# Expert results of a mixture-of-experts layer: written to their tokens' places and read back as blocks, in place of block writes and row gathers

## What is computed

```python
shared = silu(X @ sW1 + sb1) @ sW2 + sb2
activation = sqrt(softplus(X @ routing_W + expert_bias))
top_vals, top_idx = top_k(activation, 2)
y_e = silu(X @ rW1[e] + rb1[e]) @ rW2[e] + rb2[e]
out = layernorm(X + shared + sum of top_vals * y_e over the token's two experts)
```

## Time and profile before

| what | before |
|---|---|
| median of three runs | 2392.36 us |
| profiled execution, its own time | 2394.0 us |
| its span in the trace | 2392.2 us |
| PE busy | 2230.7 us (93%) |
| DVE busy | 1534.3 us (64%) |
| ACT busy | 883.9 us (37%) |
| POOL busy | 1113.8 us (47%) |
| moved by DMA | 233.26 MB |

### The profile page before, as it was taken

One profiled execution on the slowest core, in us unless ns is written; L12 is line 12 of the kernel. 1 busy time (PEld: TensorE's weight loads), 2 busy tenths in 40 slices (PEclk: granted clock), 3 DMA queues, 4 the chain that ended last, 5 costly groups with the idle time before them and its releaser, 6 DMA issues.

```text
span 2392.2 us, 40085 instructions
## 1 busy us (share of the span) xinstructions
PE 2230.7 (93%) x13154; PEld 1939.7 (81%) x13154; DVE 1534.3 (64%) x3594; ACT 883.9 (37%) x1887; POOL 1113.8 (47%) x1061
## 2 busy tenths in 40 slices
PE   6999999999999999999999999999869999999860
PEld 5788888888888878888888887888759999989750
DVE  5655666655556667655556667665656545888886
ACT  3333333333333333333333333333346555555420
POOL 1233343433333334644445453356355453777776
PEclk9999999999999999999999999999979999999995
DMA  4011111111111111111111111111264455998996
GB/s 164 18 41 49 36 36 45 45 36 41 49 36 36 36 45 36 45 36 41 49 36 36 45 45 36 36 36 37 93 212 151 152 154 179 307 312 298 298 310 209
DMA packets 102486, 233.26 MB, mean 98 GB/s; under 512 B 18256, under 2 KB 18768, under 8 KB 101520
## 3 DMA queue, kind: packets, MB, share of 16 engines
q1 hardware_dynamic: 75744, 157.96, 18.5%
q0 software_dynamic: 26256, 72.71, 10.5%
q10 hardware_dynamic: 288, 0.04, 0.0%
HBM read 141.11 MB, written 89.53 MB: 96 GB/s over the span
## 4 chain that ended last, share of the span: by engine, by line
PE 82%; DVE 6%; POOL 4%; issue 4%; DMA 3%; ACT 1%; SPq 0%; DVEq 0%; POOLq 0%; ACTq 0%
PE banks L107 23%; PE banks L109 23%; PE banks L108 23%; PE banks L113 7%; POOL RG L1811 2%; PE banks L709 2%; DMA RG<-ys,POS 1%; PE banks L447 1%; PE banks L546 1%; PE banks L731 1%; POOL b_small L1683 1%; DMA ys<-b_Y 1%; POOL b_XN L1799 1%; DVE xc L1055 1%; DVE W L1052 1%
## 5 line engine op out<-in xcount | busy, mean ns | idle before, releaser
L107 PE MATMUL banks<-W 128*128 128x512 f32 (+1 forms) x2040 | 752.9, 369 | 15.9 <-DVE W L1052 15.9
L109 PE MATMUL banks<-W 128*128 128x512 f32 (+1 forms) x2040 | 717.8, 352 | 0.0
L108 PE MATMUL banks<-W 128*128 128x512 f32 (+1 forms) x2040 | 716.6, 351 | 0.0
L107 PEld LDWEIGHTS banks<-W 128*128 128x128 f32 x2040 | 388.5, 190 | 67.7 <-POOL W L1683 15.0
L109 PEld LDWEIGHTS banks<-W 128*128 128x128 f32 x2040 | 387.2, 190 | 54.0
L108 PEld LDWEIGHTS banks<-W 128*128 128x128 f32 x2040 | 388.7, 191 | 50.7 <-issue 7.2
L772 ACT ACTIVATE W<-banks 128x512 fp32r<-128x512 f32 x320 | 191.0, 597 | 521.3 <-DVE banks L1052 243.3
L1683 POOL TENSOR_TENSOR W<-S,W 128x512 fp32r<-128x512 f32 x256 | 327.8, 1306 | 117.3 <-ACT W L772 117.2
L1683 POOL TENSOR_TENSOR X<-X,B 128x1024 f32<-128x1024 f32 x32 | 78.8, 2464 | 620.6 <-DMA X<-in_x 620.6
L772 ACT ACTIVATE W<-S 128x512 fp32r<-128x512 f32 (+1 forms) x288 | 180.4, 650 | 227.8 <-DVE S L1052 211.8
L1052 DVE TENSOR_TENSOR W<-banks,W 128x512 fp32r<-128x512 f32 x192 | 132.2, 688 | 172.3 <-ACT W L772 172.3
(11 more groups left out here) (156 smaller groups left out, 4433.6 us busy)
## 6 DMA issues: line engine op xcount, KB each, us to landing
ys<-b_Y SPq DMA_DIRECT2D x149, 256.0 KB
XT<-in_xT SPq DMA_DIRECT2D x32, 512.0 KB, 3.5
X<-in_x SPq DMA_DIRECT2D x32, 512.0 KB, 3.5
x1d<-X SPq DMA_DIRECT2D x64, 256.0 KB, 2.0
zd<-X SPq DMA_DIRECT2D x64, 256.0 KB, 2.0
b_Y<-zd SPq DMA_DIRECT2D x64, 256.0 KB, 5.1
out<-b_Y SPq DMA_DIRECT2D x64, 256.0 KB, 4.4
S<-in_we SPq DMA_DIRECT2D x32, 256.0 KB, 4.6
```

The lines of the kernel that those rows point to most:

```text
L107: e.matmul(o, ll, rh, start=start, stop=False, skip_group_check=True)
L108: e.matmul(o, lh, rl, start=False, stop=False, skip_group_check=True)
L109: return e.matmul(o, lh, rh, start=False, stop=stop, skip_group_check=True)
```

## The change

1. `ys` is one array: two planes of 64 x 128 rows (a row for each token, one plane for its first expert, one for its second) and behind them 149 x 128 spare rows. What POOL scatters into `ids` is now the place of the result, plane times 8192 plus the token's number (`idt` has two columns of numbers for it). An unfilled position of a slot holds the number of a spare row, put there at the start by DMAs out of an input array (`spare`) in place of zeros from SBUF.
2. `load` needs token numbers. `tokens(g)` works them out of `IDX`, with three small POOL instructions for a group, in front of the group's first load (i = 0, 63 and 118).
3. The write of a slot's result moves from SP (`store`) to POOL (`send(i-2)`): an indirect DMA that scatters `Y`'s rows to their places.
4. The two gathers of an ending move from POOL to SP (`rows`): two plain DMAs of 128 x 512 blocks. They wait for the same things as before, now on SP, between `fetch` and `store_out`.
5. Group 1's scatters in steps 29 and 30 go from six tiles each to eight; so eight of its tiles are left for phase two, not twelve.

```diff
@@ -28,7 +28,7 @@
 NL = len(LEVELS)
 NCST = 3
 GROUPS = [14, 12, 6]
-SCATTERS = [[3] * 10, [6, 6]]
+SCATTERS = [[3] * 10, [8, 8]]
...
-    k.ys = [nc.dram_tensor(f"ys{g['x']}", (g["slots"] * P, D), F32, kind="Internal").ap() for g in k.groups]
+    k.ys = nc.dram_tensor("ys", ((2 * NTL + k.n_slots) * P, D), F32, kind="Internal").ap()
...
+        k.EX, k.IDX, k.idt = sb("EX", [k.n_slots], I32), sb("IDX", [k.n_slots], I32), sb("idt", [2, NTL], I32)
+        k.TOK = sb("TOK", [k.n_slots], I32)
...
-            e.indirect_dma_start(k.ids[g["x"]], off, k.idt[:, n:n + 1], None).then_inc(k.d_scatter.sem(m), 16)
+            e.indirect_dma_start(k.ids[g["x"]], off, k.idt[:, j, n:n + 1], None).then_inc(k.d_scatter.sem(m), 16)
...
-    w.wait_ge(k.s_lev, 2)
-    w.wait_ge(k.s_ones, 1)
-    e.memset(k.RG[:, 0:k.n_slots], 0.0).then_inc(k.s_zero, 1)
...
 
+    def tokens(g):
+
+        a = slice(g["slot"], g["slot"] + g["slots"])
+        w.wait_ge(*k.d_idx.of(g["x"]))
+        n, x = k.NTL * P, 3 * g["x"]
+        e.tensor_scalar(k.TOK[:, a], k.IDX[:, a], float(n), float(-n), ALU.is_ge, ALU.mult).then_inc(k.s_tok, 1)
+        w.wait_ge(k.s_tok, x + 1)
+        tt(k.TOK[:, a], k.TOK[:, a], k.IDX[:, a], ALU.add).then_inc(k.s_tok, 1)
+        w.wait_ge(k.s_tok, x + 2)
+        e.tensor_scalar(k.TOK[:, a], k.TOK[:, a], float(n - 1), None, ALU.min).then_inc(k.s_tok, 1)
+
     def load(i):
 
         if i >= N:
             return
         g = k.items[i]
-        w.wait_ge(*k.d_idx.of(g["x"]))
+        if i == g["slot"]:
+            tokens(g)
+        w.wait_ge(k.s_tok, 3 * g["x"] + 3)
         for s, v in k.d_x1.last(g["tile"] + g["tiles"]):
             w.wait_ge(s, v)
         w.wait_ge(k.s_tp, i - XNS + 1)
@@ -1795,20 +1806,18 @@
             w.wait_ge(*split_of(k, 24 + i))
         else:
             w.wait_ge(k.s_dn1, k.NTL)
+        off = bass.IndirectOffsetOnAxis(ap=k.TOK[:, i:i + 1], axis=0)
+        e.indirect_dma_start(k.XN[i % XNS][:], None, k.x1d, off).then_inc(k.d_xs.sem(i), 16)
+
+    def send(i):
+
+        if not 0 <= i < N:
+            return
+        w.wait_ge(*k.d_idx.of(k.items[i]["x"]))
+        w.wait_ge(k.s_Y, i + 1)
+        w.wait_ge(*k.d_y.of(i - 3))
         off = bass.IndirectOffsetOnAxis(ap=k.IDX[:, i:i + 1], axis=0)
-        e.indirect_dma_start(k.XN[i % XNS][:], None, k.x1d, off).then_inc(k.d_xs.sem(i), 16)
-
-    def gather(c):
-        f = k.plan.finals[c]
-        w.wait_ge(k.s_cm, 4 * (c - 2) + 2)
-        for s, v in k.d_y.last(f.g["slot"] + f.g["slots"]):
-            w.wait_ge(s, v)
-        w.wait_ge(k.s_rt, k.rt_after["pos", last["x"]])
-        for j in range(2):
-            m = 2 * c + j
-            w.wait_ge(*k.d_gather.of(m - 4))
-            off = bass.IndirectOffsetOnAxis(ap=k.POS[:, j, f.n, :], axis=0)
-            e.indirect_dma_start(k.G[j][c % 2], None, k.ys[f.g["x"]], off).then_inc(k.d_gather.sem(m), 16)
+        e.indirect_dma_start(k.ys, off, k.Y[k.plan.buffer["item", i]][:], None).then_inc(k.d_y.sem(i), 16)
 
     def root(c):
         i = c % 2
@@ -1834,8 +1843,7 @@
         load(i + 6)
         if i - 3 in k.plan.base:
             root(k.plan.base[i - 3])
-        if i in k.plan.base:
-            gather(k.plan.base[i])
+        send(i - 2)
         if i == 24:
             weights(last)
         if i in k.plan.scatter:
...
-    w.wait_ge(k.s_zero, 1)
     for g in k.groups:
-        e.dma_start(k.ids[g["x"]].rearrange("(p s) o -> p (s o)", p=P), k.RG[:, 0:g["slots"]].bitcast(I32)).then_inc(k.d_zero, 16)
-    w.wait_ge(k.d_zero, 48)
+        e.dma_start(k.ids[g["x"]].rearrange("(p s) o -> p (s o)", p=P), a["spare"][:, g["slot"]:g["slot"] + g["slots"]]).then_inc(k.d_zero, 16)
+    w.wait_ge(k.s_lev, 2)
+    w.wait_ge(k.s_ones, 1)
     e.dma_start(k.RG[:, 0:KC * H + 2 * D], a["we"][E]).then_inc(k.d_sh, 16)
...
-    def store(i):
-        g = k.items[i]
-        w.wait_ge(k.s_Y, i + 1)
-        w.wait_ge(*k.d_y.of(i - 3))
-        rows = k.ys[g["x"]].rearrange("(p s) d -> p s d", p=P)[:, i - g["slot"], :]
-        e.dma_start(rows, k.Y[k.plan.buffer["item", i]][:]).then_inc(k.d_y.sem(i), 16)
+    def rows(c):
+
+        f = k.plan.finals[c]
+        w.wait_ge(k.s_cm, 4 * (c - 2) + 2)
+        for s, v in k.d_y.last(f.g["slot"] + f.g["slots"]):
+            w.wait_ge(s, v)
+        w.wait_ge(k.s_rt, k.rt_after["pos", k.groups[-1]["x"]])
+        for j in range(2):
+            m, at = 2 * c + j, (j * k.NTL + f.n) * P
+            w.wait_ge(*k.d_gather.of(m - 4))
+            e.dma_start(k.G[j][c % 2], k.ys[at:at + P, :]).then_inc(k.d_gather.sem(m), 16)
 
     def store_out(c):
         n = k.plan.finals[c].n
@@ -1960,8 +1973,7 @@
     for i in range(k.plan.end):
         if i in k.plan.base:
             fetch(k.plan.base[i])
-        if 0 <= i - 2 < N:
-            store(i - 2)
+            rows(k.plan.base[i])
         if i - 5 in k.plan.base:
...
-    arrays["ids"] = (np.arange(NB * NT)[None] * P + np.arange(P)[:, None]).astype(np.int32)
+    places = np.arange(2 * NB * NT)[None] * P + np.arange(P)[:, None]
+    arrays["ids"] = places.reshape(P, 2, NB * NT).astype(np.int32)
+    n_slots = groups_of(NT)[1]
+    arrays["spare"] = (2 * NB * NT * P + np.arange(n_slots)[None] * P + np.arange(P)[:, None]).astype(np.int32)
```

More of the change, by code:

```diff
@@ L197, in program @@
                   "rs", "X1", "X1hi", "X1lo", "LGc", "shhi", "shlo", "HF1", "hb1", "HS1", "HH1", "HL1", "dn1", "res", "z", "Sn", "Shi", "Slo", "B",
-                  "zero", "rt", "rta", "cum", "wt",
+                  "rt", "rta", "cum", "wt",
                   "whi", "w", "wp", "tp", "XH", "XL", "up", "HF", "hb", "HS", "HH", "HL", "dn", "Y",
-                  "cm", "crs", "o"):
+                  "cm", "crs", "o", "tok"):
             k.__setattr__("s_" + n, sem("s_" + n))
@@ L218, in program @@
         k.POS, k.WT = sb("POS", [2, NTL, 1], I32), sb("WT", [2, NTL])
-        k.EX, k.IDX, k.idt = sb("EX", [k.n_slots], I32), sb("IDX", [k.n_slots], I32), sb("idt", [NTL], I32)
+        k.EX, k.IDX, k.idt = sb("EX", [k.n_slots], I32), sb("IDX", [k.n_slots], I32), sb("idt", [2, NTL], I32)
+        k.TOK = sb("TOK", [k.n_slots], I32)
         k.mhalf = sb("mhalf", [2])
```

## The result

The changed kernel takes 2372.44 us, median of 4 runs (2370.23 to 2373.15), beside 2392.69 before (4 runs, 2389.82 to 2395.69): ratio 0.991, 95% interval 0.9898 to 0.9922. Compared again later, 2373.76 to 2390.87, ratio 0.9921 (0.9904 to 0.9938). The profiled span is 2368.4 against 2392.2, 23.8 us less.

The account below looks back on a forecast made before the run. PE was taken to bound (a) and (b), POOL's turn (c) and (d). Terms 0.4 + 0.2 - 5.9 + 1.9 - 5.3 = -8.7 took the median from 2392.36 to 2383.7 us, range 2374 to 2401.

Parts of the forecast that it names:

- (c): Slots of group 2 with endings of group 1: DMAs bind next at 4.75 us a slot; -5.9 us (0 to -12.5).
- the third rival: Scatter and plain reads are cheap for the DMAs, DVE alone binds (c); sum -17.3, 2375 us; chance 0.12.
- (d): Twelve endings of group 2 alone: 3.45 us each in place of 3.93, by latency; -5.3 us (-7.3 to 0).
- Last slot's step: From the last slot to group 2's first ending: 12.5 us in place of 10.6; +1.9 us (0 to +3.5).
- Tail: From the last scale to the end of the span: stays as it was, 0.
- (a) and (b): Slots alone, then group 1's slots with group 0's endings: PE stays the bound; 0 for each.
- (a): Slots alone: POOL falls 9 us behind with sends and tokens, under about 13 us of cover from early loads; 0.
- (b): Slots of group 1 with endings of group 0: PE stays the bound; 0 (-2.3 to +2).
- rival 2: Slower: the loop's send makes POOL the bound in (a) and (b); about 2401 us; chance 0.18.
- Steps 29 and 30: Two more tiles of scatters cost 5.1 us on POOL, mostly covered; +0.4 us (0 to +1).
- Start, tokens: Start: memset and waits removed beside the first products, 0; tokens: three small POOL instructions before the first load, +0.2 (0 to +1.1).
- Rival 1: The DMAs keep the pace in (c) and (d) and the gain is lost; about 2393 us (2389 to 2395); chance 0.20.

Follow-up runs that it names:

- x8: Changed kernel plus one unread plain write of 256 KB at each of group 1's 24 endings; stretch (c) 93.4 us, whole time not compared.
- x14: Changed kernel with the result scatter left out, SyncE storing each slot's result to a plain block; 2373.71 us, beside 2394.04 for the kernel before.
- x15: Changed kernel with the scaling of group 1's 24 endings done on 1 column of 512; 2370.27 us.
- x4: Changed kernel with the last 12 endings' root moved from POOL to ScalarE's square root and VectorE's reciprocal; 2484.24 us, in the slow conditions.
- x16: Changed kernel with scatters in steps 29 and 30 back to six and six tiles; 2377.61 us, beside 2394.04 for the kernel before.
- x11: Changed kernel with group 0's tokens made early and the last 12 endings' root off POOL; 2363.02 us, ratio 0.9881 to the kernel before.
- x13: Changed kernel with early tokens, late root off POOL, and a tile's two scatters of places in successive slots; 2476.63 us beside 2428.74 before.
- x9: The changed kernel itself, unaltered, run again for comparison; 2373.76 us against 2390.87 for the kernel before, ratio 0.9921.
- x1: Changed kernel with the result scatter left out, SyncE storing to plain blocks, in the slow conditions; stretch (c) 88.9 us, whole time not compared.
- x3: Changed kernel with plain stores from SyncE and group 1's scaling on 1 column, in the slow conditions; stretch (c) 87.2 us.

## Why the prediction was right or wrong

- *(c), -5.9 taken, -12.7 measured.* The step that failed is "So the DMAs bind next, and I take 4.75 us for a slot". The price of 3.43 us for 1 MB in the software queue was share divided by bytes; in the changed kernel's window from 2225 to 2265 us the same queue has 31.4% for 4.45 MB, 2.82 us: such a price is not fixed, and x8 moved a tenth more at the same share. DVE alone binds at 4.24 us a turn (x14, x15, x8), the case of the third rival: its -12.5 for (c) holds to 0.2 us.
- *(d), -5.3 taken, -6.4 measured.* 3.26 us an ending, the 3.27 of the earlier trace rows, which I had, and passed over for a sum of latencies. The root was the limit (x4: 2.91 without it). That it is not the -7.3 of the third rival comes from the first interval, 4.74 us.
- *Last slot's step, +1.9 taken, -0.9 measured.* The order of waits was right: the send starts 3.4 us after the result's end (2.9 taken). But it lands 3.6 us after its start, not 4.8 later, and the plain blocks, with little else moving, 2.5 us after issue, not 4.0. By the Trainium skill, DMA: Bandwidth & Descriptors, section Anatomy of one DMA, which is about software DMAs, the send's landing would be an estimate of 2.6 us; the trace doesn't agree. At 3.6 us it lies between that and the 4.8 of the rows. (2.2 us less than 4.8 make the whole sum -10.9, not the -11.1 that the prediction has.) In x14 the store was issued 2.0 us sooner after the result than the send, and landed 5.9 us after its issue: nothing won.
- *Tail, 0 taken, -3.1 measured.* "The end itself, last scale to the end, stays" is the second step that failed, a term put at nothing without a reason: POOL's closing DRAIN went from 9.60 to 6.50 us. It was not in my views, because they leave such instructions out. Only the gap of 9 us behind the last scale could have shown it.
- *(a) and (b), 0 taken, -1.9.* Cover and backlog in (a) are as worked out, 0.29 us of wait for PE; some slots at 59 to 62 cost about 1.1 us (x14). (b)'s 46 slots take 2.8 us less, 3.48 each, a little beyond the bound of -2.3 that I gave for 3.49. The send is 0.99 us and its gap 0.30, together 1.29 where I took 1.27; rival 2 needed a send of 1.5.
- *Steps 29 and 30, +0.4 taken.* DVE's addition in step 29 came 0.3 us later against its neighbours, and 0.1 or less was left by 1640 us; but what the edit is for escaped me (x16): I put a price on it and no worth.
- *Start, tokens +0.2 taken.* Tokens take 1.9 us where POOL had nothing else in hand; slot 0 comes 1.3 us later in one pair and 5.5 in the other. Matching ScalarE's instructions one by one shows that the first number is flattered: the changed kernel's trace was 3.4 us ahead at 100 us, the second pair's 0.2 behind. From there to slot 0 the change costs 4.7 and 5.3 us. 2.7 of them are lost between 908 and 917 us, in phase one, in a place that the prediction doesn't have, and 1.7 to 2.1 from 1740 us on, where the tokens stand. The scans of the routing on DVE, PE's wait behind them and the clock, in the changed kernel and then in x11:
```profile
901.26 2.71 DVE L1345 TENSOR_TENSOR_SCAN RG<-onesb,RG 128x28 f32<-128x28 bf16 x8
908.18 0.56 PE L107 MATMUL banks<-WS,X1l 128*128 128x264 f32 x1 [2.67 <-DVE X1l L1053]
895.00:925.00 30.00, 27.33 (x148) 23.29 (x147) 21.64 (x77) 7.94 (x17) 8.36 (x6) 0.94 0.08 27
...
901.73 1.33 DVE L1355 TENSOR_TENSOR_SCAN RG<-onesb,RG 128x28 f32<-128x28 bf16 x8
907.28 0.36 PE L108 MATMUL banks<-WS,X1l 128*128 128x264 f32 x1 [1.30 <-DVE X1l L1063]
895.00:925.00 30.00, 28.70 (x161) 24.25 (x161) 21.55 (x81) 8.48 (x19) 8.53 (x6) 1.00 0.10 36
```
The same eight scans take 1.4 us more (the first 0.87 us and the last 1.28, where they are else 0.58 and 0.19); PE waits 2.7 us in place of 1.3, and its products behind the wait start 0.22 us apart in place of 0.12, the lower level of the clock. This stands in all 14 traces of the changed kernel and its variants without the late root, and in none of the three of the kernel before and the three with the late root (x4, x11, x13), tokens early or not. So of the 5.5 us by which x11's slot 0 is ahead of x9's, 1.9 were there at 100 us, 2.7 are these scans and the clock behind them, a loss that is absent with the late root's edit, though in phase one that edit adds only a constant, and about 1 is left for the early tokens. Why the scans are longer is open.

Rival 1 fell with (c). Had (c) been taken at DVE's turn and (d) at the earlier trace rows, the sum would have been -17.3, and the drain's -3.1 half of what is then missing from the 23.8.

## What to carry to other kernels

When the busiest helper is relieved, ask what the next engine's own turn is, and read it where it already runs without a wait; that row was right to 0.02 us in (c) and (d), while the DMA bound made from shares was wrong by a tenth and took 6.6 us off the forecast. An edit that looks like tuning beside the change (eight and eight) may be what makes the change affordable: follow the backlog to the next long instruction on the same queue, not only to the end of its own stretch. And look behind the last result: the end of a span can be a drain of an engine long done.

## What the runs showed of the hardware

- POOL's closing DRAIN lasts 6.3 to 6.6 us in all kernels with sends, 8.28 without, 9.60 before, whenever it begins, and ends the span if POOL works to the end.
- A DMA share of 1.00 at 353 GB/s; 394 GB/s at a share of 1.03.
- A scatter of 128 rows of 2 KB costs POOL 0.99 us to issue, as a gather does (medians of 149), and 1.10 in the turns of (c), where DVE never idles. The root's power takes 1.05 us there, and 0.57 at 2319.71 us, where DVE stands still.
- Behind 2.7 us (near 908 us in the changed kernel) and 3.2 us (x16) in which PE had nothing to do, its products started 0.22 and 0.21 us apart in place of 0.12, at the lower level of the clock: 1.3 and 1.7 us on top of the waits.
- Unexplained: when the kernel before took 2425 to 2438 us, the kernels with sends on POOL took 2473 to 2497, by the medians 2.0 to 2.7% more than the kernel before, and the two without (x1, x3) 2396 to 2401. Slot 0 comes 20 to 30 us late in all of them; those with sends lose another 68 to 84 us in slots 0 to 71, where POOL scatters numbers as well, and 14 to 22 in slots 71 to 126; (c) and (d) are within 1 us of the others. Their traces lack 20 to 42 records each of PE and of ScalarE in phase one that the others have, so what stood still can't be read from them. The same chips gave both kinds of times, so theory D of x9, that it is the chip, falls, and x11, near 2363 with two of the edits, speaks against its theory E, that it is the edits. No trace of the kernel before was taken there. The gain shown above holds for ordinary conditions only.
